# A block's first transposed state is copied between the two halves of a decay, and block 4's chunk products stand after its third transposes

## What is computed

```python
def step(S, xs):
    q_t, k_t, v_t, a_t, b_t = xs
    Sk = jnp.einsum('bhvk,bhk->bhv', S, k_t)
    S = a_t[..., None] * S - (b_t[..., None] * (Sk - v_t))[..., None] * k_t[:, :, None, :]
    o_t = jnp.einsum('bhvk,bhk->bhv', S, q_t)
    return (S, o_t)
```

## Time and profile before

| | us |
|---|---|
| median of 3 runs | 2471.77 |
| fastest and slowest of them | 2469.62 to 2477.05 |
| the profiled execution's own time | 2463.8 |
| its span from first to last instruction | 2462.1 |

### The profile page before, as it was taken

The page is one execution under the profiler, slowest core; times in us unless marked ns, Lnnn a source line. Parts: engine busy times, 40 slices in busy tenths (PEclk is TensorE's granted clock), DMA queues, the critical chain, the costliest instruction groups (busy, mean ns, idle before and its releaser), DMA issues.

```text
span 2462.1 us, 61434 instructions
## 1 busy us (share of the span) xinstructions
PE 2090.6 (85%) x21890; PEld 1593.0 (65%) x21890; DVE 1934.0 (79%) x4382; ACT 1230.7 (50%) x2692; POOL 578.7 (24%) x577
## 2 busy tenths in 40 slices
PE   6999999999976788787787887887787877867999
PEld 4444888888865666666666765766666666743566
DVE  4222799999995898887988887978878988986676
ACT  3000687877763555554545544545545544533332
POOL 0000244444441222222222221222222222222000
PEclk9999999999987889988989889889889889887999
DMA  7000277777778565565556555655655545566540
GB/s 257 9 9 9 90 272 266 269 262 262 264 273 290 189 219 188 188 217 188 181 186 223 180 192 190 203 181 203 204 184 202 192 157 195 191 204 237 214 154 18
DMA packets 229473, 468.45 MB, mean 190 GB/s; under 512 B 48432, under 2 KB 172328, under 8 KB 199640
## 3 DMA queue, kind: packets, MB, share of 16 engines
q1 hardware_dynamic: 226184, 454.06, 53.3%
q10 hardware_dynamic: 2976, 10.72, 1.2%
q0 software_dynamic: 48, 0.16, 0.0%
HBM read 316.36 MB, written 149.57 MB: 189 GB/s over the span
## 4 chain that ended last, share of the span: by engine, by line
PE 40%; DVE 21%; issue 20%; ACT 9%; DMA 4%; POOL 2%; DVEq 1%; ACTq 1%; SPq 1%; POOLq 0%
DVE arena L1057 10%; PE PS L1495 7%; PE PS L1654 5%; ACT arena L849 4%; PE PS L1364 3%; PE PS L1437 3%; PE PS L1573 3%; PE PS L1534 2%; PE PS L1387 2%; PE PS L1481 2%; DVE arena L1148 2%; DVE arena L1156 2%; PE PS L1522 2%; PE PS L1377 2%; PE PS L1367 2%
## 5 line engine op out<-in xcount | busy, mean ns | idle before, releaser
L1387 PE MATMUL PS<-arena 128*128 x2048 | 463.7, 386 | 1.8 <-DVEq L1042 0.9
L1057 DVE SCALAR_TENSOR_TENSOR arena<-PS,SM,arena 128x256 f32<-128x256 f32 x1152 | 452.9, 476 | 15.5 <-ACT arena L719 15.5
L1387 PEld LDWEIGHTS PS<-arena 128*128 128x128 f32 x2048 | 383.4, 188 | 82.1 <-DVE arena L1057 6.5
L1495 PE MATMUL PS<-arena 128*128 128x128 f32 x1920 | 331.2, 325 | 84.9 <-ACT arena L856 84.5
L627 POOL TENSOR_TENSOR arena<-arena 128x256 f32<-128x256 f32 x128 | 115.0, 899 | 1102.7 <-DVE arena L1163 1102.7
L1495 PEld LDWEIGHTS PS<-arena 128*128 128x128 f32 x1920 | 280.1, 224 | 126.7 <-ACT arena L856 100.3
L849 ACT ACTIVATE arena<-arena 128x128 f32<-128x128 f32 x960 | 302.1, 395 | 0.0
L719 ACT ACTIVATE arena<-PS,SM 128x256 f32<-128x256 f32 x384 | 209.9, 565 | 88.9 <-PE PS L1387 84.1
L865 ACT COPY arena<-PS 128x256 f32<-128x256 f32 x240 | 89.6, 373 | 266.1 <-PE PS L1495 265.2
L1102 DVE TENSOR_TENSOR arena<-arena,PS 128x512 f32<-128x512 f32 x192 | 127.5, 685 | 117.3 <-PE PS L1534 114.4
L1481 PE MATMUL PS<-ident,arena 128*128 128x128 f32 x960 | 176.6, 314 | 28.7 <-ACT arena L849 27.3
(11 more groups left out here) (135 smaller groups left out, 3289.3 us busy)
## 6 DMA issues: line engine op xcount, KB each, us to landing
arena<-g_d SPq DMA_DIRECT2D x126, 1024.0 KB, 5.3
arena<-vas_d SPq DMA_DIRECT2D x124, 384.0 KB, 3.2
vas_d<-arena SPq DMA_DIRECT2D x32, 1024.0 KB, 11.4
kq_d<-arena SPq DMA_DIRECT2D x8, 4096.0 KB, 11.5
arena<-kq_d SPq DMA_DIRECT2D x14, 2048.0 KB, 8.0
arena<-beta_d SPq DMA_DIRECT2D x8, 2048.0 KB, 9.2
kb_d<-arena SPq DMA_DIRECT2D x8, 2048.0 KB, 10.3
vas_d<-arena SPq DMA_DIRECT2D x8, 2048.0 KB, 12.4
```

Source lines behind the costliest of these rows:

```text
L1057: nc.vector.scalar_tensor_tensor(acc, raw[:, :, i:i + PT_], CW[:, w, i, hh:hh + 1], acc, ALU.mult, ALU.add).then_inc(job_free if i == TAPS ...
L1387: ins = mm(dst.rearrange("p (b n) -> p b n", b=B), W4[:, w, kt, DH * h:DH * (h + 1)], XNT[:, kt, :, bass.ds(c * PT_ + (HALO - halo), halo ...
L1495: ins = mm(bank(7)[:, 128 * gi:128 * (gi + 1)].rearrange("v (l x) -> v l x", l=NB), STR[:, s % 2, gi, :], KQ[d][:, :, p0:p0 + 2].rearrange ...
```

## The change

Three things are written in another order, all in `chunk` of the recurrence.

First, on ScalarE, in every block with reads, the second slot's `decay` is cut into its first two tiles and its last two. `state_copy` of the block's first slot stands between the halves, where it stood behind the whole decay. `s_scaled` is raised at the end of the second half.

Second, in blocks 1, 3, 5 and 6 `key_copy` moves from ahead of the second decay to behind its second half, and so also behind the first state copy.

Third, in the two blocks with three reads (4 and 6) the third slot's decay stands behind the second state copy and no longer behind the first. In block 4 the chunk products "g2" stand on TensorE between the third slot's transposes and its reads, no longer between the second's, and ScalarE copies them out one slot later too. In block 6 the "kt" copy stays where it was.

```diff
-                def decay(s):
+                def decay(s, pairs=range(4)):
                     j, g0 = slot_pairs(s)
-                    act.wait_ge(s_updated, n * 16 + s + 1)
-                    for gi in range(4):
+                    if pairs[0] == 0:
+                        act.wait_ge(s_updated, n * 16 + s + 1)
+                    for gi in pairs:
                         p = 4 * (g0 + gi) + j
                         ins = nc.scalar.mul(S[:, p, :], S[:, p, :], EX[c][:, 6, p:p + 1])
-                    ins.then_inc(s_scaled, 1)
+                    if pairs[-1] == 3:
+                        ins.then_inc(s_scaled, 1)
...
                     if reads:
                         decay(reads[0])
-                    if keys:
+                    if keys and not reads:
                         act.wait_ge(corr_full, n * 9 + 2 + m)
-                        if m == 3:
-                            act.wait_ge(kb_in[d], (i + c) * 16 + 16)
-                        key_copy(c if m == 1 else d, *keys)
+                        key_copy(c, *keys)
                     for k, s in enumerate(reads):
-                        if k == 0 and len(reads) > 1:
-                            decay(reads[1])
+                        if k == 0:
+                            decay(reads[1], range(0, 2))
                         state_copy(s)
-                        if k == 0 and len(reads) > 2:
+                        if k == 0:
+                            decay(reads[1], range(2, 4))
+                            if keys:
+                                act.wait_ge(corr_full, n * 9 + 2 + m)
+                                if m == 3:
+                                    act.wait_ge(kb_in[d], (i + c) * 16 + 16)
+                                key_copy(c if m == 1 else d, *keys)
+                        if k == 1 and len(reads) > 2:
                             decay(reads[2])
-                        if k > 0 and m not in (1, 3):
+                        if k > (1 if m == 4 else 0) and m not in (1, 3):
                             next_evac()
                         read_copy(s)
...
                         state_transposes(s)
                         if k == 0 and updates:
                             update(updates[0])
-                        elif preps:
+                        elif preps and not (m == 4 and k == 1):
                             prep(m, *preps.pop(0))
                         reads_of(s)
```

## The result

The changed kernel took 2431.61 us, the median of four runs (2423.00 to 2436.34), against 2470.69 for the kernel before on the same chip (2469.02 to 2477.05): a ratio of 0.9833, interval 0.9808 to 0.9858. It is faster by 39 us, where some 61 were forecast. The time lies in the stated range of 2388 to 2440, but not in the band of 2397 to 2423 that was given 0.55; it lies in the next one, 2423 to 2464, which was given 0.20. Measured once more, again beside the kernel before, it took 2422.28 us against 2473.96, ratio 0.9766 (0.9708 to 0.9824). The two measurements of one and the same kernel lie 0.7% apart, so less than that between two kernels that were not measured side by side on one chip is not told. "The first execution" and "the second" are the profiled ones of these two measurements.

A forecast was written before the change was run, and what follows sets the result against it. VectorE, which carries the recurrence, idles 114.4 us ahead of `level_sub` waiting for TensorE's corrections; 0.6 + 0.28 + 0.6 + 1.05 + 1.6 = 4.1 us a chunk, 62 us over 15 chunks, gives 2410 us, range 2388 to 2440.

The forecast's parts named there:

- The sum: Blocks 1, 3, 4, 5 and 6 together win 4.1 us a chunk, 62 us over 15 chunks with reads.
- the wait behind block 6 near 1.7 us: Sign of being wrong: VectorE's wait behind block 6 stays near 1.7 us.
- new idle time in block 0: Sign of being wrong: new VectorE idle time in block 0, where gates and queues could take back the gain.
- Block 1, 0.6: Copy between the decay halves lets block 1's first reads start up to 0.96 us earlier; 0.6 us a chunk taken.
- The clock gives more: Rival: denser block 1 work keeps 2.4 GHz, all waits in blocks 1 to 6 go, 5.8 us a chunk, 2385; chance 0.17.
- Block 3, 0.28: The same copy edit frees block 3's reads and wins all of VectorE's small wait, 0.28 us a chunk.
- Block 4, 0.6: Reads and transposes fill TensorE's 2.70 us wait ahead of the chunk products; VectorE wins 0.6 us on average.
- Block 5, 1.05: The "gl" products come in time, so VectorE's wait at block 5's key mask goes: 1.05 us a chunk.
- Block 6, 1.6: Block 6's corrections come 1.5 to 2.0 us earlier by VectorE's time, against 1.7 us idle: 1.6 us won.
- Block 6 keeps its wait: Rival: new TensorE idle in block 5 brings half clock, most of block 6's 1.6 us lost, 2437; chance 0.20.
- Block 0, nothing: VectorE's idle time in block 0, behind the early gates, was left out because no edit stands there.

The follow-up runs named there:

- e8: Changed kernel plus six matmuls with unused results ahead of block 5's correction transposes on TensorE: 2413.43 us, ratio 0.9754.
- e1: Changed kernel with block 4's chunk products and their copy back at the second slot, the rest as changed: 2429.15 us, ratio 0.9794.
- e2: Kernel before with only block 4's move: chunk products behind the third transposes, copied out one slot later: 2454.71 us, ratio 0.9925.
- e4: Changed kernel plus three matmuls with unused results ahead of block 5's correction transposes on TensorE: 2415.10 us, ratio 0.9745.
- e5: Changed kernel with block 6's key transposes' copy one slot later on ScalarE, behind the third state copy: 2411.39 us, ratio 0.9722.
- e6: Changed kernel with the key copies of blocks 1, 3, 5 and 6 back ahead of the second decay: 2414.31 us, ratio 0.9742.
- e7_all: Changed kernel with SyncE's store waits a block later, six extra matmuls in block 5, block 6's key transposes' copy later: 2406.34 us, ratio 0.9725.

## Why the prediction was right and wrong

The sum was 4.1 us a chunk, and the two executions of the changed kernel gave 2.1 and 2.6 by the length from block 0's results to those of the next chunk's block 0 (94.2 us before, 92.1 and 91.7 after). Of the signs of being wrong that the prediction named, one came true in both executions, the wait behind block 6 near 1.7 us, and one in the first alone, new idle time in block 0. Term by term, by the fall of VectorE's idle time:

- **Block 1, 0.6: mis-sized, it gave 1.64 and 0.96.** The 0.96 us ahead of the reads were read rightly and are gone. The step that failed is that the clock was left as it was, and put apart as a rival: with the reads closed up to the update they ran at 2.4 GHz in 11 and in 6 chunks instead of 2, which is 0.9 us more where it happens. Why in these chunks, the runs don't tell. So "The clock gives more" came true in block 1, in part.
- **Block 3, 0.28: gave nothing in one execution and 0.08 in the other.** The idle time stayed at 0.35 and 0.19 against 0.27. The block as a whole got 0.06 and 0.22 us shorter. The assumption that all of a small wait goes with the earlier copy had no row of its own.
- **Block 4, 0.6: right, 0.51 and 0.56.** The wait ahead of the chunk products fell from the 2.70 us of the earlier trace rows to 0.18 in the same chunk 8.
- **Block 5, 1.05: right, 1.07 and 0.89** at the mask, and the block is 1.3 us shorter. In block 5 itself nothing of the wait is left.
- **Block 6, 1.6: the step that failed. It gave 0.26 and -0.23.** The sum took the reads at 1.16 us as in the earlier trace rows, because block 6 had a clock of 1.00 from end to end. But it had it behind a TensorE that was busy through block 5. The forecast itself put TensorE 2 us ahead there, and named the idle stretch only in the rival "Block 6 keeps its wait". That rival is what happened: e8 changes nothing but the hole and gets the 1.6 us. e1 shows that without the move in block 4 the loss doesn't come; with the move alone (e2) it comes as well, but in ten of 15 chunks by low stretches that have no such hole ahead of them. The rival was priced at 2437 with block 1 giving nothing; block 1 gave more than the sum had, and in the first execution block 0 took that back. That the time came out at 2432, near the rival's price and inside the range, is luck of two errors against each other.
- **Block 0, nothing: open.** The first execution lost 1.6 us a chunk there, the second 0.14, and of the other kernels with the same SyncE program e4 and e5 lost 1.0 and 1.5 while e6 and e8 lost 0.1 at most.

On the clock the rule cited in the prediction (the Trainium skill, TensorE: Matmul & The Clock Gate, section "Why this matters for your kernels"), that idle gaps between bursts bring the lower clock back, spoke on the right side for block 6: 2.11 us of idle time, then 6.8 us at 0.50, and no low stretch behind block 5's results in any chunk once the hole is filled. That rival deserved more than 0.20. But the page's own row is about longer gaps than this one, so it doesn't foretell these 2.1 us, and it doesn't say which hole does it. In chunk 1 of the changed kernel a hole of 2.10 us in the same place is followed by a clock of 1.00, and of the 15 holes of 2.7 us in block 4 before, two were followed by a block at 0.50 from end to end.

What stays open: why in one chunk the same hole is followed by the low clock and in the next not, what brings the low stretches of e2 where there is no hole, and what made the three long waits in block 0 of the first execution. Also where the rest of the gain of e7_all is. Its profiled span, 2403.3 us, is only 17.8 us under that of the changed kernel's second execution, though VectorE is idle ahead of `level_sub` for 28.6 us less (65.7 against 94.3).

## What to carry over

A forecast of time won on TensorE must take the clock with it: where the engine gets ahead, ask where it now stands idle and what runs right behind that, and price those matmuls at both rates. Two parts that make the same engine early need not add up, so measure each alone: here no difference between the copy alone and both could be told. And where an idle stretch can't be avoided, a few spare matmuls in it can be cheaper than the half rate behind it, as in block 6 here.

## What the runs showed of the hardware

- Of the 21 holes of 2.07 to 2.37 us on TensorE ahead of block 5's correction transposes, 11 in the first execution and 10 in the second, 18 were followed by a clock of 0.50 for 6.8 us or more, and 3 by none. Six spare matmuls in their place, 2.75 us, kept 1.00 in 15 of 15 chunks. With three, nine holes of 0.8 to 1.1 us were left, and six were followed by the low clock.
- Block 1's first reads ran at the full clock, in 1.16 us and not 2.07, in 2 chunks of the kernel before, where a wait of up to 1.0 us stood ahead of them, and without that wait in 11 and 6. So the clock came back in part of the chunks; the runs don't separate the wait from the rest.
- SyncE stood for 545 of 1490 us in 118 waits for stores, up to 10.4 us each. Moving these waits a block later left 48 us of them, put others in their place (971 us of all waits became 961), and moved the time by nothing that can be told. The order of one large load in that same queue went with 16 us on the same chip.
- One kernel gave 0.9833 and 0.9766 of the same kernel before in two measurements, with intervals of 0.0050 and 0.0116 that overlap only between 0.9808 and 0.9824.
